# A hybrid attention and feed-forward block on one core: the next stage's first layer in halves inside a drain, unread transposes in TensorE's rests, other PSUM banks for one chunk

## The reference

```python
x = x + attn_a(_layernorm(x), ...)   # 16 heads of 16, 4 key/value heads, softmax over 2048 keys
x = x + ffn(_layernorm(x), ...)
x = x + attn_b(_layernorm(x), ...)   # linear attention: silu, rope, causal, no softmax, gate, norm, Wo
x = x + ffn(_layernorm(x), ...)
```

```python
gf = _global_net(x.mean(axis=1, keepdims=True), ...)
out = x
for _ in range(3):
    h = _gelu(out @ w1 + b1); h = _gelu(h @ w2 + b2); h = _gelu(h @ w3 + b3)
    tf = sigmoid(h @ w4 + b4)
    coupling = 0.1 + adaptive_range * (0.7 * gf + 0.3 * tf - 0.5) * 2.0
    out = out + coupling * _twist(out)
```

## Time and profile before

| | us |
|---|---|
| median of 3 runs | 2059.12 (2056.25 to 2059.63) |
| profiled execution | 2055.61 |
| its span | 2053.8 |
| busy: PE, DVE, ACT, POOL | 1959.6, 1807.0, 1490.4, 204.7 |

### The profile page before, as it was taken

The page is one execution under the profiler, slowest core; times in us unless marked ns, Lnnn a source line. Parts: engine busy times, 40 slices in busy tenths (PEclk is TensorE's granted clock), DMA queues, the critical chain, the costliest instruction groups (busy, mean ns, idle before and its releaser), DMA issues. The chain is left out here.

```text
span 2053.8 us, 47783 instructions
## 1 busy us (share of the span) xinstructions
PE 1959.6 (95%) x14944; PEld 795.4 (39%) x14944; DVE 1807.0 (88%) x3351; ACT 1490.4 (73%) x2934; POOL 204.7 (10%) x442
## 2 busy tenths in 40 slices
PE   7999999999999999999999999989998899997995
PEld 4323333333333333333333333324433566665432
DVE  7899999999999999999999999975458699997348
ACT  5348888888888888888888888864556565645757
POOL 2310000000000000000000000032013111122012
PEclk9879999999999999999999999999999999999998
DMA  5431221121122112212211211222000000000002
GB/s 161 125 99 48 68 65 44 51 73 51 44 66 65 44 49 72 54 44 66 65 44 49 72 54 44 56 72 108 23 1 2 1 2 2 3 2 1 1 1 83
DMA packets 110303, 101.33 MB, mean 49 GB/s; under 512 B 52288, under 2 KB 91520, under 8 KB 110192
## 3 DMA queue, kind: packets, MB, share of 16 engines
q1 hardware_dynamic: 110192, 99.97, 17.6%
HBM read 78.84 MB, written 20.77 MB: 49 GB/s over the span
## 5 line engine op out<-in xcount | busy, mean ns | idle before, releaser
L1545 DVE TENSOR_REDUCE mx<-ps 128x1 f32<-128x512 f32 x2048 | 1273.8, 683 | 12.6 <-PE ps L688 8.4
L1149 ACT ACTIVATE YT<-ps 128x512 f32<-128x512 f32 x2048 | 1056.7, 602 | 255.3 <-PE ps L742 255.3
L713 PE MATMUL ps<-YT,work 128*32 128x512 f32 x4096 | 546.2, 605 | 0.0
L688 PE MATMUL ps<-work 64*128 64x512 bf16 x2048 | 456.7, 390 | 5.1 <-DVE mx L1545 3.4
L736 PE MATMUL ps<-work 64*128 64x512 bf16 x2048 | 395.0, 378 | 0.1
L742 PE MATMUL ps<-work 34*128 34x512 bf16 x2048 | 394.1, 378 | 0.0
L688 PEld LDWEIGHTS ps<-work 64*128 64x128 bf16 x2048 | 144.6, 93 | 612.5 <-DVE mx L1545 538.8
L736 PEld LDWEIGHTS ps<-work 64*128 64x128 bf16 x2048 | 142.5, 94 | 83.9 <-ACT YT L1149 16.8
L742 PEld LDWEIGHTS ps<-work 34*128 34x128 bf16 x2048 | 100.6, 94 | 78.3 <-issue 1.4
L713 PEld LDWEIGHTS ps<-YT,work 128*32 128x32 f32 x4096 | 80.7, 108 | 120.5 <-ACT YT L1149 113.3
L844 PE MATMUL ps<-work,c_s 128*128 128x512 f32 x192 | 96.3, 625 | 16.5 <-ACT work L1207 11.3
(11 more groups left out here) (185 smaller groups left out, 1795.0 us busy)
## 6 DMA issues: line engine op xcount, KB each, us to landing
work<-k_scr SPq DMA_DIRECT2D x640, 64.0 KB, 2.1
work<-q_scr SPq DMA_DIRECT2D x640, 32.0 KB, 1.7
o_scr<-o_sb SPq DMA_DIRECT2D x32, 256.0 KB, 2.2
X<-in_L_attn_a_x_dram SPq DMA_DIRECT2D x8, 512.0 KB, 7.2
work<-negt SPq DMA_DIRECT2D x256, 1.0 KB
work<-o_scr SPq DMA_DIRECT2D x16, 256.0 KB
work<-inv_scr SPq DMA_DIRECT2D x16, 256.0 KB
out_dram<-X SPq DMA_DIRECT2D x8, 512.0 KB, 2.9
```

What stands on the lines that cost most here:

```text
L688: mm(ps[:, bank_of[x], :], qa[rows, p, jp, qt * P:(qt + 1) * P], ka[rows, p, kc_ * CH:(kc_ + 1) * CH], start=True, stop=True).then_inc(a_m ...
L713: m = mm(ps[32 * j:32 * j + 32, 7, :], vst[:, p, t, :], prob(GROUP * t + j), start=t == 0, stop=t == KTILES - 1)
L1149: fn(prob(u), ps[:, S_BANK + u % S_RING, :], ACT.Exp, scale=HD ** -0.5).then_inc(exp_ok, 1)
L1545: dve.tensor_reduce(mx[:, p, at_:at_ + 1], ps[:, bank_of[x], :], AX_X, ALU.max).then_inc(a_max, 1)
```

## The change

Five edits. (1) Chunk 1's first layer in cycle 0 goes to banks 3 and 4, in both feed-forwards (`first_bank_of`). (2) `repeat(times)` issues transposes of the identity to bank 7, which nothing reads: 14, 8 and 8 in the drain of the first feed-forward, 14 and 8 in that of the second. (3) In the drain of the tiles `turn_chunk(3, 1)` moves behind `norm_turn(31)`, and the first layer of the second feed-forward's item 0 is done in two halves, `first_half(0)` (bank 0) and `first_half(1)` (bank 1), between the last tiles' work; `feed_forward(1)` then skips item 0's first layer. (4) Chunks 1 and 2 of that stage are normalised by VectorE (`scaled`) at n = 32 and 33 and not by ScalarE (`spread`). (5) Two waits on n_xn keep the order between the two engines.

```diff
--- before.py
+++ after.py
@@ -405,6 +405,10 @@
 
             return 5 * (n % 2) if ORDER[n][0] == 1 else 0
 
+        def first_bank_of(n):
+
+            return 3 if n == 1 else first_bank(n)
+
         def is_item(n):
 
             return 0 <= n < SLOTS and ORDER[n] is not None
@@ -819,7 +823,7 @@
                 def first(n):
 
                     y, c = ORDER[n]
-                    b_ = first_bank(n)
+                    b_ = first_bank_of(n)
                     if y == 0:
                         pe.wait_ge(n_y, 2 * ((2 * k + 1) * NCH + c + 1))
                         w = c1_s
@@ -867,6 +871,11 @@
                             m = mm(ps[:, 4 - o, :], c4_s[rows, :], h3[rows, slot, :], start=True, stop=True)
                     m.then_inc(f_z, 1)
 
+                def repeat(times):
+
+                    for t in range(times):
+                        pe.transpose(ps[:, 7, t % 4 * P:(t % 4 + 1) * P], ident[:], ident[:])
+
                 st = 2 * k + 1
                 if k == 0:
                     turn_chunk(st, 0)
@@ -876,7 +885,7 @@
                     for b in range(BATCH):
                         if 0 <= n - GLOBAL_AT[b] < 3:
                             global_net(n - GLOBAL_AT[b], b)
-                    if ORDER[n][0] < CYCLES - 1:
+                    if ORDER[n][0] < CYCLES - 1 and (k == 0 or n > 0):
                         first(n)
                     if n >= 1:
                         second(n - 1)
@@ -894,6 +903,7 @@
 
                 if k == 0:
                     fourth(LAST - 3)
+                    repeat(14)
                     second(LAST)
                     second(LAST + 1)
                     third(LAST - 1)
@@ -903,12 +913,14 @@
                     third(LAST + 1)
                     second(LAST + 4)
                     fourth(LAST + 1)
+                    repeat(8)
                     third(LAST + 3)
                     second(LAST + 5)
                     pe.wait_ge(f_d, NCH)
                     pe.wait_ge(f_ga, 6)
                     turn_chunk(2, 0)
                     fourth(LAST + 3)
+                    repeat(8)
                     project_qk(0, 0)
                     second(LAST + 6)
                     pe.wait_ge(n_y, 2 * (2 * NCH + 1))
@@ -1049,6 +1063,18 @@
                     m = mm(ps[:, 1, 0:DIM], on_t[:, p, kt, :], lo_s[:, kt, :], start=kt == 0, stop=kt == KT - 1)
                 m.then_inc(l_w, 1)
 
+            def first_half(mt):
+
+                pe.wait_ge(n_y, 2 * (3 * NCH + 1))
+                if mt == 0:
+                    pe.wait_ge(l_r, TILES)
+                else:
+                    pe.wait_ge(l_x, TILES)
+                for kt in range(KT):
+                    m = mm(ps[:, mt, :], c1_s[:, kt, mt * P:(mt + 1) * P], YT[:, kt, ch(0)], start=kt == 0, stop=kt == KT - 1)
+                if mt == KT - 1:
+                    m.then_inc(f_h1, 1)
+
             def pipeline(n, p, place):
                 if is_tile(n):
                     energy(n, p)
@@ -1057,7 +1083,6 @@
                 if n == TILES:
                     pe.wait_ge(l_em, 4 * TILES)
                     turn_chunk(3, 0)
-                    turn_chunk(3, 1)
                 if is_tile(n + 1):
                     project_vg(n + 1, 1 - p)
                 if is_tile(n + 2):
@@ -1072,8 +1097,14 @@
                     turn_chunk(2, ROWS_AT[n])
                 if is_tile(n - 2):
                     out_proj(n - 2, p)
+                if n == TILES:
+                    first_half(0)
                 if is_tile(n - 1):
                     norm_turn(n - 1, 1 - p)
+                if n == TILES:
+                    turn_chunk(3, 1)
+                if n == TILES + 1:
+                    first_half(1)
                 if n in ROWS_AT:
                     pe.wait_ge(n_y, 2 * (2 * NCH + ROWS_AT[n] + 1))
 
@@ -1162,6 +1193,8 @@
                 g = st * NCH + c
                 act.wait_ge(n_sh, g - NCH + 1)
                 act.wait_ge(n_t, 2 * (g - 1))
+                if (st, c) == (3, 3):
+                    act.wait_ge(n_xn, g)
                 for t in range(4):
                     m = fn(xn[:, c % 2, t], X[:, 4 * c + t, :], ACT.Identity, bias=shift4[:, c, t:t + 1], scale=root4[:, c, t:t + 1])
                 m.then_inc(n_xn, 1)
@@ -1195,11 +1228,12 @@
                         act.wait_ge(f_up, k * 2 * NCH + updates(n + 1))
                     wait(act, f_h2, base + n - 1)
                     for mt in range(KT):
-                        m = fn(h1[:, n % 2, mt, :], ps[:, mt, :] if y == 0 else summed(c)[:, mt, :], ACT.Gelu,
+                        m = fn(h1[:, n % 2, mt, :], ps[:, first_bank_of(n) + mt, :] if y == 0 else summed(c)[:, mt, :], ACT.Gelu,
                                bias=bias[:, D1 + mt:D1 + mt + 1])
                     m.then_inc(f_a1, 1)
                     if y == 0:
-                        act.copy(summed(c), ps[:, 0:KT, :]).then_inc(f_as, 1)
+                        b_ = first_bank_of(n)
+                        act.copy(summed(c), ps[:, b_:b_ + KT, :]).then_inc(f_as, 1)
 
                 def second(n):
                     act.wait_ge(f_h2, base + n + 1)
@@ -1398,19 +1432,16 @@
                         gates(n // 4)
                 if n in ROWS_AT:
                     put_rows(2, ROWS_AT[n])
-                if n == TILES:
-                    put_rows(3, 0)
-                    put_rows(3, 1)
+                if n >= TILES:
+                    put_rows(3, n - TILES)
                 if is_tile(n - 1):
                     affine(n - 1, 1 - p)
                 if n in SPREAD_AT:
                     spread(2, SPREAD_AT[n])
                 if n in TURNED_AT:
                     turned_rows(0, TURNED_AT[n])
-                if n in (TILES - 2, TILES - 1):
-                    spread(3, n - TILES + 2)
-                if n == TILES + 1:
-                    spread(3, 2)
+                if n == TILES - 2:
+                    spread(3, 0)
 
             feed_forward(0)
 
@@ -1459,6 +1490,8 @@
                 g = st * NCH + c
                 dve.wait_ge(n_rs, g + 1)
                 wait(dve, n_t, 2 * (g - 1))
+                if (st, c) == (3, 1):
+                    dve.wait_ge(n_xn, g)
                 for t in range(4):
                     m = dve.tensor_scalar(xn[:, c % 2, t], X[:, 4 * c + t, :], moments[:, c, t, 0:1], root4[:, c, t:t + 1],
                                           ALU.subtract, ALU.mult)
@@ -1833,6 +1866,8 @@
                     state(n, n % TPB == TPB - 1)
                 if is_tile(n - 2):
                     residual(n - 2)
+                if n >= TILES:
+                    scaled(3, n - TILES + 1)
                 if n in MINUS_AT:
                     turned_minus(0, MINUS_AT[n])
                 if n in JOINED_AT:
```

## The result

| | before | after |
|---|---|---|
| median us | 2057.9 (2056.25 to 2059.63, 4 runs) | 2039.9 (2039.0 to 2043.47, 4 runs) |
| span of the profiled execution | 2053.8 | 2037.6 |
| its mean granted clock | 0.975 | 0.983 |
| busy: PE, DVE, ACT | 1959.6, 1807.0, 1490.4 | 1952.1, 1808.9, 1485.5 |

The ratio is 0.9916 (95%: 0.9899 to 0.9933), some 17 us less. Of the 16.2 us between the spans, 1.61 were there before any changed instruction (the first transposes behind the attention start at 1436.25 before and 1434.64 after). 14.59 us are left for the change, where my sum was 15.5.

What follows compares the result with a forecast made beforehand. TensorE was taken as busy nearly everywhere, losing time to waits and low clock in four short stretches. 4.4 + 3.1 + 7.1 + 0.9 = 15.5 us off the 2059.12 median gave 2043.6 (likeliest 2043.5), range 2038.5 to 2050.5.

Steps and rivals of the forecast that it cites:

- The head: First feed-forward's start: with other banks, chunk 1's first layer skips the copy wait; chunk 2's starts 4.4 us earlier.
- the shift travels on: Behind the first head, TensorE is busy without rests for some 70 us, so the 4.4 us gain carries on.
- rival E: Early starts are given back to a sum for global_net or to ScalarE in the second feed-forward: 2055.1 us, chance 0.05.
- `global_net`'s operand: Behind the first head: the operand is there at about 1454.4 and TensorE asks at 1455.3.
- The unread transposes: Feed-forward drains: they keep TensorE's clock up through rests, gaining 3.1 us in the first and 0.9 in the last.
- rival B: Unread transposes don't hold the clock in the drains, which then give nothing: 2048.5 us, chance 0.12.
- ScalarE's wait of 3.60: First drain, at 1590.76: this wait was the room for the 3.1 us gain and would be gone.
- The tile drain: End of the tile stage: halves, reordering and VectorE's normalising start chunk 2's first layer 7.1 us earlier.
- Rival C: The clock falls in the rebuilt tile drain all the same, through pieces of rest: 2046 us, chance 0.14.
- the clock at 2.5 us: Tile drain: TensorE's gain from clock, 0.75 + 1.77 us, counted beside its gain from waits.
- The last drain: Second feed-forward's drain: ScalarE's 0.91 us wait goes, VectorE starts 0.9 us earlier and bounds the end; later eight bring nothing.
- 2043.5: Whole kernel: the likeliest time in us, forecast against the median of the kernel before, 2059.12.

Runs made afterwards that it cites:

- e0: The changed kernel run once more, unaltered, as the measure for its group; median 2042.2 us, ratio 0.9933 to the kernel before.
- e1: The changed kernel without its 52 unread transposes; median 2047.65 us, ratio 0.9962 to the kernel before.
- e4: The changed kernel with every two unread transposes replaced by one unread float32 matmul; median 2039.06 us, ratio 0.9927 to the kernel before.
- e6: The changed kernel with chunks 1 and 2 normalised by ScalarE again, the halves kept; median 2042.24 us, ratio 0.9931 to the kernel before.
- e9: The kernel before with only the other banks for chunk 1's first layer, in both feed-forwards; median 2050.55 us, ratio 0.9967.
- e10: The changed kernel without the three groups of eight unread transposes, the fourteens kept; median 2042.84 us, ratio 0.993 to the kernel before.
- e7: The changed kernel with twice the unread transposes, 28 for 14 and 16 for 8; median 2040.23 us, ratio 0.9919 to the kernel before.
- e2: The changed kernel with chunk 1's first layer in its old banks, in both feed-forwards; median 2043.48 us, ratio 0.9941 to the kernel before.
- e3: The kernel before with only the 52 unread transposes added; median 2048.94 us, ratio 0.9966.
- e5: The kernel before with only the rebuilt tile drain, old banks and no unread transposes; median 2048.01 us, ratio 0.9961.

## Why the prediction was right, step by step

**The head (4.4 us).** 4.76 at chunk 2's first layer, with the mechanism as written. Wrong was "the shift travels on": 1.63 of it went at item 12, whose rest of 2.88 I had used as proof that a rest needn't bring the clock down. Of the eight traces with the other banks and nothing in that rest, seven have this second layer at 3.41 to 3.75 us (changed, e0, e1, e4, e6, e9, e10) and one at 1.96 (e7); in those of before, e2, e3 and e5, with the old banks, it took 1.95 or 1.96. Without fills in the drain behind it, more is lost: A gains only 0.93 by the banks (before to e9) and 0.81 (e5 to e1), with fills 2.97 (e2 to changed). Nor is TensorE without rests behind the head, as I wrote: ahead of the transposes at 1471.48 it waits 1.38 us for VectorE. That rest moved along (1465.26 after), so it cost little: 4.61 of the 4.76 reach item 12. What went there is a part of rival E, the early start given back, by the clock and not by a wait. `global_net`'s operand, which I put 0.9 us ahead of the need, is 0.09 ahead.

**The unread transposes (3.1 and 0.9 us).** They hold the clock; rival B has no support in any trace (e1, e3, e4, e10). The Trainium skill's page "TensorE: Matmul & The Clock Gate", section "Part 4: PE-mode transpose", says that full rate does not engage for transposes; here L848 behind fourteen of them took 1.98 us, not 3.40, and the measurement decides. And the fills themselves ran at full rate: eight took 1.07 us at 1578.17, where eight transposes at the low clock take 1.79. The sizes fit the trace from which they were worked out, 3.09 and 1.07 in e3, and are too small for the changed kernel: 6 to 9.5 us (e1). Two reasons that runs show: without the fills it has more low matmuls in both drains to save than the earlier trace rows had (e1), and the projection, where I gave the eight no gain, is one of them: L955 took 3.78 us in e10, which leaves out both eights of this drain, and L958 1.98 in the changed kernel. For e3, which has the old banks, neither holds; why its ratio gives 7.0 us (its group's medians 5.3) and its distances 4.3 stays open. Wrong was that ScalarE's wait of 3.60 would be gone: it became 1.95.

**The tile drain (7.1 us).** 7.50 in C, and the tile-drain edits alone 6.47 (e5). The step through the halves holds to a few tenths: the transposes of chunk 1, which I put 4.5 us behind chunk 0's (1879.6 to 1884.1), are at 4.37 (1876.34 - 1871.97), and the rests sum to 1.4 us for my 1.5. Chunk 2's first layer waits for ScalarE's copy, as written. Rival C did not come. What I told wrongly is who earns it: I put the clock at 2.5 us (0.75 + 1.77), and some 3.4 of the 7.50 are the clock that had been down in the earlier trace rows, which e9 also got back without any new order. What I left out is the output projection between, 1.92 us before (1884.53) and 1.03 in e9, with the turn behind it. Whether the new order keeps it up was not settled: of the three traces with the old order two had the low clock there (before, e3), of the eleven with the new one none, but for chunk 0's transposes in e1 (1.71 us), where a low stretch from further ahead ran on. The move of the normalising to VectorE is worth 2.1 of the rest (e6), the halves 1.0, the banks 1.0.

**The last drain (0.9 us).** 1.07 in e3, 1.09 in the changed kernel; the later eight bring nothing there (e10).

**The point.** 15.5 against 14.59 in the traces. The parts differ more than their sum: A gave 6.04 us for my 7.5 (4.4 + 3.1), C 7.50 for 7.1, D 1.09 for 0.9, B -0.04. Another 1.61 us between the two profiled executions lie ahead of the change: that start lies anywhere from 1433.39 to 1436.52 us in the fourteen traces, which don't differ ahead of it. 2043.5 lies 3.6 us above the measured 2039.9, because I added the 3.5 us by which the median of before stood above its profiled execution. The changed kernel has 2039.9 for a profiled 2039.44. That is in part luck: in e0 it has 2042.2 for a profiled 2039.93, and the median of before lay anywhere from 2054.25 to 2057.97 in the three groups. Whether the changed kernel has less to add, having fewer rests that can bring the clock down, is not shown.

## What to carry to other kernels

A rest of 1.8 to 2.9 us in TensorE can cost twice, as a wait and as the clock behind it; which of several rests brings the clock down changed with the edits ahead of them, so a gain ahead of them can be given back at the next one, and parts measured alone (7.0, 8.0 and 6.8 us for fills, tile drain and banks) need not sum to the whole (14 to 17). The distances show both ways: in C the tile drain and the banks alone give 6.47 and 4.40 us, together 7.50, since both get back the same low clock; in A the fills and the banks alone give 3.09 and 0.93, together 6.04. My advice from this, not an experiment: fill such rests with unread work first, then move the waits. Here a fill that outlasted its rest by 0.45 us left 0.35 at the next stage (e7), and three groups of eight left out gave back 2.6 us (e10 against e7) to 3.7 (A to D).

## What had not been expected of the hardware

- The same rest of 2.88 us ahead of the same instruction left the second layer at 1.96 us (before, e2, e3, e5) or 3.41 to 3.75 us (changed, e0, e1, e4, e6, e9, e10), and these arrive some 4.6 us earlier (92.20 us behind the first transposes, not 96.81) and have no low clock in the head. In e7, as early (92.34), it took 1.96. What decides it stays open.
- B is 284.66 to 284.72 us in eight kernels, though the clock was not down at the same places: in before and e5 at the projection some 10 us on (L944 at 1605.03 took 3.62 us, not 1.88), in the six others behind the rest of 2.40 us at the end of the stage (the attention's second part 1.36 to 1.87 us for 1.08, the projection behind it 1.86 to 2.08 for 1.13). Equal distances don't prove an equal course.
- Unread transposes of 128x128 float32 cost 0.109 us each in a row (fourteen: 1.75 with the tail, 28: 3.27), and as a fill are worth what float32 matmuls are (e4).
